# Products on TensorE whose results nobody reads, at five places of a two-layer transformer kernel

## The reference

```python
x = x + layernorm(L0_attn(layernorm(x)))   # RMS norm, 16 heads of 16, RoPE, causal softmax, wo, residual
x = x + layernorm(L0_ffn(layernorm(x)))    # 8 experts of 16, top 2: softmax gates, silu(x down) up
x = x + layernorm(L1_attn(layernorm(x)))   # 8 heads of 32, two softmax maps per head, difference of both
x = x + layernorm(L1_ffn(layernorm(x)))    # 64 experts of 64, top 4, and two shared experts of 256
```

```python
scores = einsum('bshd,bthd->bhst', q, k) / sqrt(16)
probs = softmax(where(causal, scores, -inf)); out = einsum('bhst,bthd->bshd', probs, v)
```

## Time and profile before

| | us |
|---|---|
| median of 3 runs | 652.14 |
| lowest, highest | 641.99, 655.16 |
| profiled execution | 648.67 |
| its span (first to last instruction) | 646.9 |
| PE busy in it (share) | 467.8 (72%) |
| DVE busy | 341.4 (53%) |
| ACT busy | 234.8 (36%) |
| POOL busy | 179.5 (28%) |

### The profile page before, as it was taken

The page is one execution under the profiler, slowest core; times in us unless marked ns, Lnnn a source line. Parts: engine busy times, 40 slices in busy tenths (PEclk is TensorE's granted clock), DMA queues, the critical chain, the costliest instruction groups (busy, mean ns, idle before and its releaser), DMA issues.

```text
span 646.9 us, 8796 instructions
## 1 busy us (share of the span) xinstructions
PE 467.8 (72%) x2581; PEld 296.1 (46%) x2581; DVE 341.4 (53%) x1150; ACT 234.8 (36%) x473; POOL 179.5 (28%) x275
## 2 busy tenths in 40 slices
PE   1876759888786377779376868676669999999410
PEld 1433334433442245326245524443348888886300
DVE  5376684555434672523536136149726766663545
ACT  2222134332554164544235645342033443430215
POOL 5111012211232031321002322111165555504751
PEclk9897765555987598986868877878599999999775
DMA  6000010000000000000000300499035555533332
GB/s 201 16 2 1 8 42 0 2 1 1 0 1 2 0 2 0 17 2 0 1 0 1 99 0 2 152 390 302 7 91 158 163 161 163 163 98 123 105 103 68
DMA packets 29766, 42.82 MB, mean 66 GB/s; under 512 B 3616, under 2 KB 21024, under 8 KB 29728
## 3 DMA queue, kind: packets, MB, share of 16 engines
q1 hardware_dynamic: 25120, 29.74, 13.5%
q0 software_dynamic: 4608, 12.59, 7.4%
HBM read 31.83 MB, written 10.49 MB: 65 GB/s over the span
## 4 chain that ended last, share of the span: by engine, by line
PE 55%; DVE 21%; ACT 8%; issue 7%; POOL 5%; another core or an unknown queue 2%; DMA 2%; SPq 0%; DVEq 0%; ACTq 0%; POOLq 0%
PE PSUM L657 10%; PE PSUM L957 8%; PE PSUM L601 5%; PE PSUM L630 5%; PE PSUM L947 4%; PE PSUM L782 3%; PE PSUM L671 3%; DVE st L1236 2%; POOL QP L583 2%; PE PSUM L938 2%; PE PSUM L607 2%; DVE H L1246 2%; PE PSUM L594 2%; PE PSUM L818 1%
## 5 line engine op out<-in xcount | busy, mean ns | idle before, releaser
L1047 ACT ACTIVATE PR<-PSUM 128x1024 f32<-128x1024 f32 (+1 forms) x96 | 82.1, 880 | 83.1 <-PE PSUM L671 82.8
L536 POOL TENSOR_SCALAR_AFFINE_SELECT PR<-PR 128x256 f32<-128x256 f32 x128 | 52.9, 428 | 177.1 <-ACT PR L1047 176.4
L1317 DVE CUSTOM_DVE_ANT_0 XN<-PSUM,XN 128x128 f32<-128x128 f32 (+3 forms) x128 | 58.1, 489 | 48.4 <-PE PSUM L630 48.1
L573 POOL DMA_INDIRECT QP<-tokens,tok_of x64 | 60.8, 950 | 56.1 <-PE PSUM L938 24.1
L657 PE MATMUL PSUM<-PR,VA 128*32 128x256 f32 (+3 forms) x512 | 60.1, 566 | 12.1 <-DVE XT L1366 9.7
L957 PE MATMUL PSUM<-arena,QP 128*128 x256 | 66.0, 380 | 3.5 <-ACT QP L1196 3.5
L671 PE MATMUL PSUM<-QT,KTr 32*128 32x384 f32 (+7 forms) x256 | 53.0, 450 | 12.8 <-ACT PR L1047 10.2
L630 PE MATMUL PSUM<-KTr,QT 32*128 32x128 f32 (+3 forms) x128 | 43.4, 536 | 14.6 <-DVE mx L1317 14.2
L957 PEld LDWEIGHTS PSUM<-arena,QP 128*128 128x128 f32 x256 | 48.2, 190 | 10.6 <-issue 4.2
L404 POOL TENSOR_TENSOR QP<-QK,QP 128x128 f32<-128x128 f32 (+1 forms) x16 | 9.5, 591 | 148.2 <-ACT QP L397 80.2
L601 PE MATMUL PSUM<-wq_sb,XT 128*128 128x512 f32 x64 | 40.7, 771 | 6.6 <-DVE QK L1298 4.0
(11 more groups left out here) (238 smaller groups left out, 821.9 us busy)
## 6 DMA issues: line engine op xcount, KB each, us to landing
arena<-in_wgu SPq DMA_DIRECT2D x4, 2048.0 KB, 15.7
expert_outputs<-QP SPq DMA_DIRECT2D x64, 128.0 KB
arena<-in_wd SPq DMA_DIRECT2D x2, 2048.0 KB, 16.6
wq_sb<-in_wqkv SPq DMA_DIRECT2D x2, 768.0 KB, 5.4
X<-in_x SPq DMA_DIRECT2D x2, 512.0 KB, 4.6
QP<-in_wsgu SPq DMA_DIRECT2D x1, 1024.0 KB, 5.4
tokens<-XN SPq DMA_DIRECT2D x2, 512.0 KB, 12.8
QP<-tokens,tok_of POOLq DMA_INDIRECT x64
```

The source lines that it names most:

```text
L536: ins = pool.affine_select(diag, diag, [[0, 2], [1, P]], ALU.is_ge, 0.0, base=0, channel_multiplier=-1)
L573: pool.indirect_dma_start(out=XG[:, i % U, :], out_offset=None, in_=h_dram, in_offset=bass.IndirectOffsetOnAxis(ap=tok_of[:, i:i + 1], axis=0)
L1047: did(sc.activation(PR[:, n % PSLOTS, 2 * half:2 * half + 2, 0:WIDTH[chunk]], PSUM[:, 2 * half:2 * half + 2, 0:WIDTH[chunk]], ACT.Exp, sca ...
L1317: did(dv.tensor_tensor_reduce(MSK[m % 2][:, 0:nk], o[:, 0:nk], MASKQ[:, S - nk:S], op0=ALU.add, op1=ALU.max, scale=1.0, scalar=NEG, accum_ ...
```

## The change

Products are added on PE at five places. Their results go to banks whose content is overwritten or was read before; none is read, and no semaphore is raised by them. `keep(n, o)` issues n products of `ident` and `up_sb` (256 columns) into bank o.

1. In `max_beside`, ahead of each of batch 1's 64 maxima and behind its wait, a product of `ident` and `ident` (128 columns) into the maximum's own bank.
2. In the opening, 3, 3, 3 and 8 of `keep` behind pairs 28, 29, 30 and 31 of batch 0's maxima, into bank 4. Before the first stand waits for the projections' reads and for the weights.
3. Another 3 behind the opening, after two of its waits.
4. In `after0`, at step 28 (behind the up products), 32 into bank 0, for both batches, after a wait for the last exponentials of the batch's attention.
5. In `after1` for batch 1, at step 5 (behind the shared experts 0 and 1), 8 into bank 5.

```diff
+KEEP_AT = {28: 3, 29: 3, 30: 3, 31: 8}
...
+            def keep(n, o):
+                for _ in range(n):
+                    pe.matmul(o[:, 0:D], ident[:, :], up_sb[:, :], start=True, stop=True)
...
                     if kind == "max":
+                        pe.matmul(bank(6 + k % 2)[:, 0:P], ident[:, :], ident[:, :], start=True, stop=True)
                         maxima(1, n, bank(6 + k % 2))
...
+                if step == UP + 1:
+                    pe.wait_ge(s_p, (b + 2) * STEPS)
+                    keep(32, bank(0))
                 if step == TURN2:
                     turn_tokens(2, b, 6)
...
+                if b and step == OUT1 + TB + 1:
+                    keep(8, bank(5))
                 if step == TURN3:
                     turn_tokens(3, b, 6)
...
                     for m in (2 * n, 2 * n + 1):
                         maxima(0, m, bank(m % 4))
+                    if n in KEEP_AT:
+                        if n == min(KEEP_AT):
+                            pe.wait_ge(s_qkve, NT)
+                            pe.wait_ge(s_w0, 64)
+                        keep(KEEP_AT[n], bank(4))
             pe.wait_ge(s_tev, 2 * NT)
             pe.wait_ge(s_qkve, NT)
+            keep(3, bank(4))
             pe.wait_ge(s_const, 2)
```

## The result

The changed kernel is slower. It took 687.54 us in the median of 4 runs (684.05 to 691.31), beside 651.52 us (641.99 to 655.16, 4 runs) for the kernel before; the ratio is 1.0637 with a 95% interval of 1.0461 to 1.0813. The forecast was 641 with a range of 629 to 660. Over the whole study the executions of the kernel before fall into two groups, 636 to 644 and 648 to 655 us; medians are made with both, the ratios of the experiments against the shorter one, and 1.0637 rests on one run of either (641.99 and 650.91), which makes it rather too small.

What follows compares the result with a forecast made beforehand. The prediction took the stage with batch 1's maxima as bound by a nearly full PE at 1.2 GHz; 1.7 - 7.8 + 0.4 - 1.2 - 1.7 = -8.6 from 648.67 gave 640.1, set at 641 us for run variation, range 629 to 660.

Steps and rivals of the forecast that it cites:

- the stage's -7.8: Batch 0's attention with batch 1's maxima between: at a mostly high clock it gets 7.8 us shorter, to near 60.
- The price of a product in the stage: Ahead of batch 1's maxima: a 128-column float32 product costs 0.27 us at 2.4 GHz and 0.50 at 1.2.
- the +3.5: Upper bound for the stage's 32 loops: 0.16 us gained against 0.27 added in each, 3.5 us longer in all.
- That the clock mostly stays at 2.4 GHz: Stage with batch 1's maxima: clock starts at 2.4 GHz and mostly stays, as the next stage holds 0.85.
- -10.3 from weighing and turns: Pieces that hold PE in the stage: weighing shrinks by 8.6 us and four turns by 1.7.
- +2.5 for the loops: The stage's loops of maxima with the new products: 2.5 us longer, taken between bounds of -0.6 and +3.5.
- The opening, +1.7: In front of the stage: twenty added products put its start at 94.35 us instead of 92.65.
- Behind the up products, +0.4 and -1.2: After each batch's up products: 32 products overrun the hole, later work runs faster; batch 0 +0.4 us, batch 1 -1.2.
- ahead of the routing, -1.7: Before the second routing: 8 products raise the clock, routing products take some 1.9 us instead of 3.67, 1.7 gained.
- The clock stays low in the stage: Rival: the stage stays at 1.2 GHz, 64 products by 0.50 us, +23 to +32, kernel 671 to 680; chance 0.10.
- The clock falls in the stretches between weighings: Rival: with a quarter to a third of the stage low, its gain is used up, kernel 645 to 652; chance 0.25.
- The stage is as fast as its neighbour: Rival: the stage takes 51 to 53 us, 15 to 17 gained, kernel 631 to 634; chance 0.20.

Runs made afterwards that it cites:

- the grouped kernel: Changed kernel with the same 64 128-column products, those of a step issued together ahead of its first maximum: 661.33 us, ratio 1.0323.
- the wide products: Changed kernel with a 256-column product instead of a 128-column one ahead of each of the 64 maxima: 660.7 us, ratio 1.0344.
- The kernel with 48 wide products: Changed kernel with 48 256-column products in bursts, three per step without weighing, instead of one ahead of each maximum: 651.01 us, ratio 1.0104.

## Why the prediction was wrong, point by point

- **What bounds the kernel** was read rightly: the stage at 1.2 GHz, PE nearly full, little idle time. The consequence wasn't drawn. A stage with 8.85 us of idle PE in 67.8 was given 64 more products.
- **Two steps of the stage's -7.8 failed**, the clock's level and the price of a product, and it measured +44.0. By the estimate above, 68.5 us at the high clock, the price accounts for some 8 of the 52 us between the forecast stage of 60.0 and the measured 111.8, and the low clock, with the higher price that a product has there, for some 43. By the same estimate the kernel would have come out near 650 with the price wrong and the clock right, inside the range.
- **The price of a product in the stage** failed: it took the gain away. It was taken from products "among other weights", 0.27 and 0.50 us. Those stand in a train of full-height products; the grouped kernel has 0.29 for the same. Between 32-row products the change's own cost 0.42 and 0.73. The prediction had the warning beside it: two maxima share 0.50 us, so a maximum is cheap only because it lies beside its neighbour, and a product that lets nothing lie beside it costs that as well. Besides, the sum let one product into each of 32 loops, but a loop carries two maxima and so two products. With a widest maximum at 0.42 (152.36 to 152.78 with the wide products) an estimate is 2 by 0.42 + 0.42, or 1.68 us of PE in a loop of 1.56: PE would have set it, and not DVE. The Trainium skill's "TensorE: Matmul & The Clock Gate", part 3, on when a weight load runs ahead, was put down as leaning to the +3.5. The traces agree in that a full-height product shares little with the 32-row ones around it: it lasts 0.49 us, and the maximum behind it starts 0.42 after it. That a train of full-height products comes cheaper, at 0.29, doesn't follow from that rule; the runs show it.
- **That the clock mostly stays at 2.4 GHz** is the step that took the time out of the range: it was there for 3.9 of 111.8 us. It was inferred from the next attention's 0.85 with fewer full-array products. That stretch turned out to be no fixed thing, 0.69 to 0.85 in the profiles with the same instructions. The wide products held the clock for 79 of 82 us and the narrow ones didn't, with PE busy for 98 and 99% of the stage. So the weight in the sum belonged to a clock that nothing in the trace promised. Why the clock falls with the one and not with the other stays open.
- **-7.8 for the stage at a high clock** was too good as well. The kernel with 48 wide products is the nearest case to it, 68.0 of 71.37 us at 2.4 GHz, and its stage is 3.5 us longer than before. The step "-10.3 from weighing and turns" holds in size: weighing went from 19.6 to 10.9 us, 8.7 where the sum has 8.6, and PE's own work fell by 26.8, near the 29.5 that halving gave. What the products cost was the mis-sized term: 27.2 us of PE in that kernel. The change's own 64 at 0.42 would be 26.9 even at 2.4 GHz, where the prediction's bounds have 17.3 and its sum only +2.5 for the loops with the products in them.
- **The opening, +1.7**, was +1.4; all of it ran at 2.4 GHz as the prediction took it. That it came so close is in part luck: the stage began between 92.7 and 97.1 us in the six profiles with the twenty products, and between 91.0 and 95.1 in the eight without, 2.4 us apart in the mean.
- **Behind the up products, +0.4 and -1.2**, were +0.3 and -1.3; **ahead of the routing, -1.7**, was -1.7. There the products do stand in a train behind full-height ones, and the price of 0.43 held (32 in 13.8 us). Timeline of PE in the changed kernel, batch 0:

```profile
254.47 13.98 PE L639 MATMUL PSUM<-up_sb,ident 128*128 128x256 f32 x64
268.28 1.04 PE L596 MATMUL PSUM<-ident,XN 128*128 128x128 f32 x8
270.58 1.96 PE L603 MATMUL PSUM<-wq_sb,XT 128*128 128x512 f32 x4 [1.26 <-ACT XT L1044]
```

- **The rivals.** "The clock stays low in the stage" named the mechanism, a full PE at 1.2 GHz, and had a chance of 0.10 and a price of +23 to +32. The stage measured +44: 64 by 0.73 is 46.7 where it had 64 by 0.50. Its own reason "against", that twenty products stood in front, bought 3.9 us. The range ended at 660 because this rival was left out of it. "The clock falls in the stretches between weighings" had a quarter to a third of the stage low, where it was 97%. "The stage is as fast as its neighbour" (51 to 53 us) holds for no kernel, the high clock given: 71.4 and 81.9 us.

## What to carry to other kernels

Price an added instruction by the company it will stand in: the same float32 product cost 0.27 to 0.29 us in a train of full-height products and 0.42 alone among 32-row ones (0.73 at the low clock), and there the 32-row neighbours lose their overlap. Before paying with PE work for a higher clock, ask how much idle PE the stage has to pay from: in a hole the products are free and the work behind it runs at 2.4 GHz (7 us here by the stretches, with counts sized to the holes). In a stage that is 87% busy they took back all that the clock gave, and the narrow ones of the change didn't even raise it. And where the sum rests on a clock level that no row of the kernel shows for that stage, the low-clock case belongs inside the range.

## What the runs showed of the hardware that was not expected

- A PE that is busy for 99% of a stage of 112 us was granted 1.2 GHz for 108 of them (the changed kernel), and one busy for 98% of 82 us was granted 2.4 GHz for 79 (256 instead of 128 columns in the product). PE's busy time alone didn't tell the one from the other.
- Height and type set the price of a product among 32-row ones, at equal columns: 0.10, 0.23 and 0.73 us added to the stage for 32 rows in float32, 128 rows in bf16, 128 rows in float32.
- The same instructions of one attention took 45.3 to 55.0 us in different kernels, by where the clock fell. A gain of a few us elsewhere is hidden by this until many runs are compared. What moves the fall from one kernel to the next stays open.
